# A language-model tower on one core: weight turns ahead of head sums in the first block's attention, V's projection ahead of Q's and K's turns

## The reference

```python
h = rms_norm(rms_norm(emb[x]) * norm_w @ proj.T)            # depends on the token id alone
n = layernorm(h)
q, k = feature_map(n @ Wq.T), feature_map(n @ Wk.T)         # per head: * gamma + beta, layernorm
v = n @ Wv.T                                                # 16 heads of 32
a = where(causal, (q @ k.T / 32**0.5) ** 2, 0)
h = h + ((a @ v) / (a.sum(-1) + 1e-5)) @ Wo.T
n = layernorm(h)
y = fwht(n * SU_ug) / 64                                    # Walsh-Hadamard over 512
y = silu(y @ W_gate.T * s_g) * (y @ W_up.T * s_u)           # 2048 wide
out = h + fwht(y * SU_dp) / 64 @ W_down.T * s_d
```

## Time and profile before

| | us |
|---|---|
| median of 3 executions (lowest, highest) | 1351.8 (1349.68, 1355.08) |
| the profiled execution, its own time | 1351.9 |
| its span in the profile | 1350.0 |
| TensorE, VectorE, ScalarE, GpSimd busy | 1236.2, 646.8, 418.5, 568.2 |
| head sums of quads 0, 1, 2, 3 begin at | 64.32, 77.45, 90.11, 102.94 |
| first row sum of the tail begins at | 115.20 |
| first feed-forward matmul begins at | 148.22 |

### The profile page before, as it was taken

The page is one execution under the profiler, slowest core; times in us unless marked ns, Lnnn a source line. Parts: engine busy times, 40 slices in busy tenths (PEclk is TensorE's granted clock), DMA queues, the critical chain, the costliest instruction groups (busy, mean ns, idle before and its releaser), DMA issues.

```text
span 1350.0 us, 18434 instructions
## 1 busy us (share of the span) xinstructions
PE 1236.2 (92%) x7065; PEld 591.2 (44%) x7065; DVE 646.8 (48%) x1136; ACT 418.5 (31%) x731; POOL 568.2 (42%) x487
## 2 busy tenths in 40 slices
PE   6765787677999999999999999999999999999999
PEld 3452333233444444444444444444444444444444
DVE  2668457654465355536354545544553555361110
ACT  4663675251143213321233023311331133211210
POOL 0552265522176416642475237531764166411210
PEclk9887788788999999999999999999999999999999
DMA  9800033272353244523452344424533345120000
GB/s 330 320 1 1 16 71 71 47 133 55 96 112 83 63 95 103 109 48 94 109 110 56 86 100 108 73 71 99 104 79 71 86 112 99 21 76 14 1 1 32
DMA packets 231043, 113.17 MB, mean 84 GB/s; under 512 B 209412, under 2 KB 210744, under 8 KB 230456
## 3 DMA queue, kind: packets, MB, share of 16 engines
q1 hardware_dynamic: 219776, 77.78, 26.4%
q0 software_dynamic: 10240, 33.56, 8.4%
q10 hardware_dynamic: 952, 0.75, 0.2%
HBM read 53.08 MB, written 9.70 MB: 46 GB/s over the span
## 4 chain that ended last, share of the span: by engine, by line
PE 73%; DVE 7%; DMA 6%; ACT 4%; issue 4%; POOL 4%; SPq 0%; DVEq 0%; ACTq 0%; POOLq 0%
PE bank L1357 22%; PE bank L1358 22%; PE bank L1359 22%; PE bank L1515 3%; DMA prod<-sg 3%; DMA wgu<-h 1%; POOL h L509 1%; POOL hid L565 1%; DMA wd<-h 1%; ACT wgu L1099 1%; DMA xT<-in_L_tok_proj_weight 1%; PE bank L1552 1%; PE bank L1350 1%; ACT xT L1099 1%; DVE xT L910 1%
## 5 line engine op out<-in xcount | busy, mean ns | idle before, releaser
L1357 PE MATMUL bank<-xT,wgu 128*128 128x512 f16 x1024 | 391.3, 382 | 1.4 <-DVE xT L910 1.4
L1358 PE MATMUL bank<-xT,wgu 128*128 128x512 f16 x1024 | 391.3, 382 | 0.0
L1359 PE MATMUL bank<-xT,wgu 128*128 128x512 f16 x1024 | 390.8, 382 | 0.0
L565 POOL TENSOR_TENSOR hid<-a,hid 128x512 f16<-128x512 f32 x128 | 176.4, 1378 | 261.8 <-ACT hid L1099 261.4
L994 DVE SCALAR_TENSOR_TENSOR a<-bank,kap,sg 128x512 f32<-128x512 f32 x128 | 96.0, 750 | 335.7 <-PE bank L1359 291.3
L1357 PE MATMUL bank<-wd,hid 128*128 128x512 f16 x512 | 195.2, 381 | 0.0
L1358 PE MATMUL bank<-wd,hid 128*128 128x512 f16 x512 | 195.0, 381 | 0.0
L1359 PE MATMUL bank<-wd,hid 128*128 128x512 f16 x512 | 195.0, 381 | 0.0
L1359 PEld LDWEIGHTS bank<-xT,wgu 128*128 128x128 f16 x1024 | 100.8, 98 | 122.9 <-issue 3.6
L1357 PEld LDWEIGHTS bank<-xT,wgu 128*128 128x128 f16 x1024 | 101.0, 99 | 121.8 <-issue 3.9
L1358 PEld LDWEIGHTS bank<-xT,wgu 128*128 128x128 f16 x1024 | 100.8, 98 | 119.1 <-issue 3.3
(11 more groups left out here) (203 smaller groups left out, 1398.6 us busy)
## 6 DMA issues: line engine op xcount, KB each, us to landing
out<-a SPq DMA_DIRECT2D x24, 256.0 KB, 2.2
wgu<-in_L_ffn_W_gate SPq DMA_DIRECT2D x4, 1024.0 KB, 15.4
wgu<-in_L_ffn_W_up SPq DMA_DIRECT2D x4, 1024.0 KB, 15.5
wd<-in_L_ffn_W_down SPq DMA_DIRECT2D x4, 1024.0 KB, 15.3
out<-h_row SPq DMA_DIRECT2D x8, 256.0 KB, 2.0
hid<-att_table,ids_p POOLq DMA_INDIRECT x72, 3.5
xT<-in_L_tok_proj_weight SPq DMA_DIRECT2D x1, 1024.0 KB, 10.3
p<-in_L_attn_Wq SPq DMA_DIRECT2D x1, 1024.0 KB, 13.0
```

The costliest lines, as they stand in the source:

```text
L565: nc.gpsimd.tensor_tensor(hid[:, 1, s, :], a32[:, :], hid[:, 0, s, :], ALU.subtract)\
L1357: mm(dst, w[0], v[0], start=first, stop=False)
L1358: mm(dst, w[0], v[1], start=False, stop=False)
L1359: return mm(dst, w[1], v[0], start=False, stop=final)
```

## The change

It changes the written order on two engines, in block 0's attention alone, and moves one projection. On TensorE `attend` is split in two: `picks` (with the counts of later blocks) and `sums` (head sums, flips, and later blocks' mixes and Wo rows). For other blocks `attend` calls one after the other, as before. For block 0 a slot is now pick, Wo's small sum (slot 9), turn of the unit or of the Wo quarter, and only then head sums or flip. On VectorE `attend_first`, the division of a quad's heads, now stands ahead of the slot's low half and diagonal. V's projection moves from behind slot 0's picks to ahead of `qk_turn(0)`. No instruction, wait or DMA is added or taken away; ScalarE, GpSimd and SyncE keep their order.

```diff
@@ VectorE, slots of block 0
                 if s == 2:
                     val_low()
+                attend_first(s)
                 for x in units_before(s - 1):
                     unit_low(x)
                 if s - 1 in WO_UNIT_AT:
                     wo_low(WO_UNIT_AT.index(s - 1))
                 for x in units_before(s + 1):
                     unit_diagonal(x)
-                attend_first(s)
@@ TensorE, ahead of the slots
+            pe.wait_ge(S["t_copied"], 16)
+            for k in range(DC):
+                last = mm(QKV[2][:, :], xTf[:, k * P:(k + 1) * P], small_t[3][:, k, :], start=(k == 0), stop=(k == DC - 1))
+            last.then_inc(S["v_ready"], 1)
             qk_turn(0)
             qk_turn(1)
@@
-            def value():
-                pe.wait_ge(S["t_copied"], 16)
-                for k in range(DC):
-                    last = mm(QKV[2][:, :], xTf[:, k * P:(k + 1) * P], small_t[3][:, k, :], start=(k == 0), stop=(k == DC - 1))
-                last.then_inc(S["v_ready"], 1)
@@
-            def attend(n, s):
+            def picks(n, s):
...
+            def sums(n, s):
                 heads_at, wo_at, mix_at = (HEADS_AT0, (), ()) if first(n) else (SUMS_AT, WO_AT, X_MIX_AT)
...
+            def attend(n, s):
+                picks(n, s)
+                sums(n, s)
@@ TensorE, slots of block 0
             for s in range(SLOTS0):
-                attend(0, s)
-                if s == 0:
-                    value()
+                picks(0, s)
                 if s == 9:
                     wo_sum()
                 for x in units_before(s):
                     unit_turn(x)
                 if s in WO_UNIT_AT:
                     wo_turn(WO_UNIT_AT.index(s))
+                sums(0, s)
             tail()
```

## The result

The changed kernel takes 1338.11 us (median of 4; 1336.86 to 1340.19) beside 1352.95 (median of 4; 1349.68 to 1355.08) timed beside it: a ratio of 0.9894, 95% interval 0.9868 to 0.9919. Timed once more, unaltered, beside the last experiments, it took 1337.68, ratio 0.9877 (0.9853 to 0.9900). So it is faster by 1.1 to 1.2%, and the forecast of 1340.2 (1335.5 to 1345.5) holds. The profiled execution took 1338.78, its span 1337.0, against 1350.0.

A forecast was written before the change was run, and what follows sets the result against it. No engine is full in the reordered slots; engines waiting for each other set their length. Quads, end and clock 9.5, V's place 1.3, earlier clock 0.9 make 11.7: 1351.9 to 1340.2 us, range 1336 to 1344 (1335.5 to 1345.5 for the forecast).

The forecast's parts named there:

- the circle between heads and units: Block 0's quads: sums ahead of a turn, low half ahead of the division, flip ahead of the next turn; 13.13 us a quad.
- (2): Quad 1's sums to quad 2's: same chain with Wo's small sum, 0.4, ahead of the turn; 9.9 us.
- (5): Clock in the quads: 0.5 us charged for one turn at the lower clock; bounds nothing and 1.9 a quad.
- (4): Quad 3's sums to first row sum: 12.5 against 12.26 us, loss 0.25; Wo's-rows branch ends about 1 us earlier.
- (6): V's projection moved ahead of the slots: 1.3 us gained from its place, 0.9 from the clock ahead of it.
- (1): Quad 0's sums to quad 1's: turn and its high half leave the path; 9.5 us against 13.13.
- The sign that the division starts at the sums' end: VectorE in the quads: heads' division starts within 0.1 us of the sums' end if the forecast is right.
- (3): Quad 2's sums to quad 3's: Wo's turns have half the instructions, heads' high half waits for the division; 9.0 us.
- Rival B: Quads: clock falls in each gap before a flip, 5.7 us come back, gain 6, 1346 us; chance 0.14.
- Rival C: Without V's burst TensorE enters the slots at clock 0.50 and stays there; 1355 us; chance 0.03.
- Rival E: More than counted: mixing steps shrink, tail runs at a better clock; gain 15 to 16, 1336 us; chance 0.05.

The follow-up runs named there:

- the two ScalarE edits: Two runs against the changed kernel, on ScalarE: heads' high half ahead of the unit's in slots 5, 9, 13 (1336.96 us); squares ahead of the oT copy (1335.77 us).
- both orders and V left: Against the changed kernel, V's projection left in slot 0 with both new orders kept: 1340.26 us, ratio 0.9928.
- Wo's sum later: Changed kernel with ScalarE's heads and squares first, and Wo's small sum, total, power and fit one slot later: 1339.16 us, ratio 0.9892.
- diagonal early: Changed kernel with unit 1's diagonal on VectorE moved from slot 1 to slot 0: 1340.54 us, ratio 0.9900.

## Why the prediction was right, step by step

The mechanism, the circle between heads and units and its undoing by TensorE's order, is what the runs show. That the total came so near is in part luck: in the quads a miss of 0.6 in (2) met a clock charge of 0.5 in (5) that did not fall due, (4) and half of (6) were mis-sized, and the tail gave what was not in the sum.

**(1) Quad 0 to 1** was worked out at 9.5 and took 9.24; the links are those of the chain: division at +1.40 (forecast +1.4), heads' high half +3.22 (+3.4), flip +5.14 (+5.3), next high half to sums 1.91 (1.92). That TensorE's order carries it is shown by the runs with one order each. The division on VectorE, which the expectation of the run with TensorE's order alone called free, was: the heads' high half started 3.23 after the sums there. GpSimd's first power (68.97, 1.67 us) lies in this quad and not in quad 1, where the forecast had it; the two ScalarE edits ran into it here.

**(2) Quad 1 to 2,** 9.9, took 10.52 to 10.73 at full clock. The term missed is contention: I took VectorE's small instructions at their durations in the old order, where these two met no GpSimd instruction, and in a denser order they do. The sign that the division starts at the sums' end failed here for that reason: it came at 75.04, 3.00 after the sums' start instead of 1.4.

**(3) Quad 2 to 3,** 9.0, took 8.92. The sum of the quads, 28.4, measured 28.69 and 28.71: gain 9.9 where (1) to (3) and the clock charge of (5) said 9.7. The profile of before is the shortest of three in the old order (38.62, 39.09, 40.64), so 9.9 is the least that they give.

**(4) End:** forecast 0.25 longer, measured 0.31 shorter; the first mixing step met GpSimd for less long (1.74 for 2.13). The branch through Wo's rows is nearer than the 1 us that I worked out: with both orders and V left the row sum waited 0.17 us for it (end 12.17), and with TensorE's order alone it decided by 1.43, and the end was 13.26.

**(5) Clock:** the charge of 0.5 did not fall due in the changed kernel (1.00 in all quads), and in quad 1 of four other runs it did, at 0.8 to 1.5. Rival B is thus real in single executions, at no more than a quarter of its 5.7. Rival C did not come: in front the granted clock was 0.73 from 50 us to the sums, then full.

**(6) V's move:** forecast 1.3 + 0.9 = 2.2. Front took 18.17 to 19.73, mean 18.85, in the four profiles with V in slot 0; with V moved and the early slots otherwise unedited 15.61 to 17.29, mean 16.08 over eight: 2.8. Of it 0.46 is the second turn (1.80 to 1.34 from its start to the scores, in all). The scores took 2.09 in all four with V in slot 0, and 1.17 to 2.09 in the eight, mean 1.79: 0.3. So the clock ahead of the slots gave 0.8, near my 0.9, and the place freed 2.0 where I took 1.3. That term was mis-sized because I read V's projection at 4.12 us from one profile. It is the shortest of the four: the others have 4.40, 4.99 and 5.68, at the lower clock for part of it, against 3.70 in all ten profiles where it is moved. Head 2's scaling followed it, 10.81, 11.10, 11.68 and 12.37 after the scores' start. The longest, with VectorE's order alone:

```profile
52.94 5.68 PE L1470 MATMUL bank<-oT,hid 128*128 128x512 f32 x8
```

In the eight profiles with V moved it came at 8.69 to 9.32. The single profile of the changed kernel showed 0.88 in all, its diagonal having taken 2.46 and the clock being 0.73. The projection began at 38.92, not 40.7, since the sixteenth copy was done earlier in that execution, and it had long ended when the second turn came.

**Not in the sum:** the tail's 1.68. It takes about 31.35 or 33.02 us in every profile, and the difference is one group of Wo rows, at full clock or not, behind the same kind of idle stretch. In the changed kernel:

```profile
111.37 0.62 PE L1543 MATMUL bank<-c,sg 128*128 128x128 f16 x8 [2.86 <-DVE sg L904]
...
111.83 0.38 PE L1357 MATMUL bank<-wo_t,oT 128*128 128x512 f16 x1
```

and before:

```profile
123.13 0.75 PE L1539 MATMUL bank<-c,sg 128*128 128x128 f16 x8 [3.55 <-DVE sg L904]
...
123.68 0.63 PE L1357 MATMUL bank<-wo_t,oT 128*128 128x512 f16 x1
```

Either order can have either length: VectorE's order alone had 31.34, Wo's sum later 33.04. The long one came in two of three profiles of the old order and in one of eleven of the new, which is too few to say whether the new order makes it rarer. Rival E had named this and the shorter mixing step, at a chance of 0.05; both are in the changed kernel's profile, 1.68 and 0.39.

By the terms that the runs tie to the change, 9.9 + 2.8 + 0.3, it is worth 13.0 us where I said 11.7. That this is also the difference of the two spans is chance: there the front gave 0.88 only, and the tail and Q/K the rest. Measured medians lie 14.8 and 16.7 apart, with intervals of about 3.5 and 3 to each side, so the forecast gain is on the low side; what makes up the rest is open.

## What to carry to other kernels

When engines walk one list of slots, look for a chain that crosses the list twice: here heads waited for units and units for heads, on three engines. Putting the work whose inputs are ready ahead of the work that will wait, on the one engine where both queues meet, undid it; the like edit on the engine whose wait lies elsewhere in the chain did nothing for it. Before moving the next term, expect another bound within half a microsecond: of six further edits some did shorten their own link, none shortened the total by what could be measured, and one made its stretch longer. A denser order makes instructions meet that never met before, so short durations from the old trace are lower bounds.

## What the runs showed of the hardware that was not expected

- A VectorE instruction on a single column (0.16 us) took 0.96 beside a GpSimd instruction, one on 8 columns 1.01 instead of 0.12, and a 128x512 one 3.20 instead of 0.68 beside two in a row. Those that read PSUM kept 0.68. The waiting is inside the instruction's duration, not shown as idle time.
- Which of the two waits is not told by the recorded starts: in "diagonal early" VectorE's instruction starts at 53.67 and GpSimd's at 54.05, and VectorE's is the long one (3.20); with TensorE's order alone VectorE's starts at 96.06 and GpSimd's at 96.22, and GpSimd's is (2.06 instead of 1.15).
- The granted clock differs between executions of the same order: quad 1 of the changed kernel had 1.00 twice, and the same order with only the later mixing step moved took 11.64 instead of 10.53, with unit 8 turned in 2.06 us.
